# Attention's row maximum from the rounded parts of q and k, two heads at a time in row bands of the TensorE array

## The reference

```
qkv = h @ w_qkv + b_qkv                      # h: normalised and modulated x
q, k, v = rope(split(qkv)) per head          # (2, 16, 2048, 32) each
attn = softmax(q @ k^T / sqrt(32), axis=-1)  # 2048 x 2048 for each of 32 heads
out = attn @ v ;  x = x + out @ w_ao + b_ao
x = x + swiglu(norm2(x) @ w_fc + b_fc) @ w_fo + b_fo
```

## Time and profile before

| | |
|---|---|
| median of three runs | 3860.85 us |
| profiled execution, first to last instruction | 3862.3 us |
| granted TensorE clock, mean | 0.937 |
| up to the start of stage B | about 438 us |
| stage B ahead of its first product with v | 438 to 516 us |
| stage B, 32 units | 516 to 2535 us |
| stages C and D | 2535 to 3862 us |

### The profile page before, as it was taken

How to read it: one execution, slowest core, us unless ns; L and a number is a source line. 1 busy time by engine, 2 the same in 40 slices (tenths; PEclk the granted TensorE clock), 3 DMA queues, 4 the chain that set the end, 5 groups by cost and what they waited for, 6 DMA issues and landing times. The chain is left out here.

```text
span 3862.3 us, 54952 instructions
## 1 busy us (share of the span) xinstructions
PE 3485.2 (90%) x16467; PEld 2120.3 (55%) x16467; DVE 2194.5 (57%) x3311; ACT 1586.2 (41%) x2851; POOL 1691.7 (44%) x506
## 2 busy tenths in 40 slices
PE   6888699999999999999999999966399999799999
PEld 5666444444344443443443444445388888688887
DVE  2888577777677776777776767745422222221222
ACT  1433135555565555565655555523321111211111
POOL 0222247677777776777776767744200000100000
PEclk9999789999999999999999999987699999899999
DMA  4444421121210302112112031057531211322120
GB/s 172 139 140 145 127 65 26 45 52 32 65 32 24 73 26 58 39 27 70 29 29 68 25 71 28 25 175 245 174 117 49 82 43 55 98 98 76 47 83 22
DMA packets 154291, 289.31 MB, mean 75 GB/s; under 512 B 22410, under 2 KB 39930, under 8 KB 148606
## 3 DMA queue, kind: packets, MB, share of 16 engines
q1 hardware_dynamic: 139700, 250.89, 22.0%
q10 hardware_dynamic: 10512, 22.81, 1.8%
q0 software_dynamic: 3840, 12.59, 1.1%
HBM read 183.83 MB, written 102.27 MB: 74 GB/s over the span
## 5 line engine op out<-in xcount | busy, mean ns | idle before, releaser
L688 DVE TENSOR_REDUCE b_mpart<-b_m 128x1 f32<-128x512 f32 x2127 | 1334.5, 683 | 515.0 <-PE b_m L754 514.0
L675 POOL TENSOR_TENSOR b_acc<-b_acc,b_pt 128x2048 f32<-128x2048 f32 x288 | 1320.7, 4586 | 360.2 <-ACT b_pt L642 349.8
L642 ACT ACTIVATE b_pt<-b_s 128x512 f32<-128x512 f32 x2048 | 1118.6, 595 | 766.5 <-PE b_s L779 738.7
L779 PE MATMUL b_s<-b_qs,b_ks 98*128 98x512 f32 x2050 | 898.2, 438 | 89.8 <-ACT b_pt L642 75.1
L754 PE MATMUL b_m<-b_ks,b_qs 96*128 96x512 f32 x2127 | 828.0, 436 | 46.4 <-issue 20.5
L779 PEld LDWEIGHTS b_s<-b_qs,b_ks 98*128 98x128 f32 x2050 | 398.1, 194 | 691.6 <-ACT b_pt L642 605.8
L754 PEld LDWEIGHTS b_m<-b_ks,b_qs 96*128 96x128 f32 x2127 | 410.6, 201 | 307.1 <-DVE b_mpart L688 201.2
L844 PE MATMUL b_o<-b_pt,b_vg 128*32 128x512 f32 x4096 | 557.5, 617 | 0.0
L1184 DVE SCALAR_TENSOR_TENSOR d_uf<-d_a,keep_chan,d_sg 128x512 f32<-128x512 f32 x128 | 96.0, 750 | 578.4 <-PE d_a L1212 578.4
L1136 POOL DMA_DIRECT2D d_raw<-in_w_fc x32 | 24.0, 754 | 591.4 <-POOLq L1061 495.7
L1155 ACT ACTIVATE d_sg<-d_g,keep_chan 128x512 f32<-128x512 f32 x128 | 88.1, 688 | 419.3 <-PE d_g L1212 419.3
(11 more groups left out here) (130 smaller groups left out, 3781.6 us busy)
## 6 DMA issues: line engine op xcount, KB each, us to landing
b_ks<-scratch_qk_hi SPq DMA_DIRECT2D x18, 1024.0 KB, 14.1
b_qs<-scratch_qk_hi SPq DMA_DIRECT2D x68, 256.0 KB, 4.4
scratch_qk_hi<-a_q_hi SPq DMA_DIRECT2D x64, 256.0 KB, 2.5
scratch_qk_lo<-a_q_lo SPq DMA_DIRECT2D x64, 256.0 KB, 2.8
d_h_hi<-scratch_h_hi SPq DMA_DIRECT2D x16, 1024.0 KB, 7.4
d_h_lo<-scratch_h_lo SPq DMA_DIRECT2D x16, 1024.0 KB, 9.7
d_y<-scratch_y SPq DMA_DIRECT2D x16, 1024.0 KB, 8.4
b_ks<-scratch_qk_lo SPq DMA_DIRECT2D x9, 1024.0 KB, 13.1
```

Of the source, the lines that this page charges most:

```text
L642: act.activation(pt[:, kt % RING, h, :], ps_s[:, i % LEAD, :], ACT.Exp, scale=SCALE).then_inc(p_ready, 1)
L675: pool.tensor_tensor(sums[:], a, pt[:, kt % RING, :, :], ALU.add).then_inc(pool_added, 1)
L688: dve.tensor_reduce(mpart[slot][:, i // 4, i % 4:i % 4 + 1], ps_m[:, i % EARLY, :], AX.X, ALU.max).then_inc(max_done, 1)
L779: pe.matmul(ps_s[:, i % LEAD, :], ks[kslot][0:QR, h, kt * P:(kt + 1) * P], qs[qslot][0:QR, h, :], start=True, stop=True).then_inc(st_done, 1)
```

## The change

The maxima are computed from `qk_hi` alone: 32 rows of the array for a head and not 96. Since the four heads' rows of `qk_hi` lie side by side on 128 partitions, two heads' matmuls are issued one after the other in two bands of 32 rows. Both write a PSUM bank of their own, and one DVE instruction reduces both banks (128 x 2 x 512). What was 64 items a unit is now 32 (letter `M`).

- New tiles: `kn` (keys, rounded part, two slots) and `qn` (queries, rounded part, four slots), loaded by `load_group_hi` and `load_queries_hi`. The tile `qs` has two slots and not four.
- The four banks of the maxima are two pairs (`PAIRS = 2`).
- `ORDER` is new: nearly all steps are `sMsdMss`, `TURN` is 9 and not 12.
- POOL adds one key tile less, PE takes it: a `d` in seven steps of a unit and not in six (0, 2, 4, 7, 10, 12, 15 where it was 0, 2, 4, 7, 10, 13).
- On SP, `load_queries` goes to the end of a unit's body; the new loads stand at the start of it, ahead of the group's loads.

```diff
-BY_POOL = [0, 1, 2, 4, 5, 7, 8, 10, 11, 13, 14]
+BY_POOL = [0, 1, 2, 4, 5, 7, 8, 10, 12, 13]
...
-        FIVE, FOUR, TURN = "smsdmmmsms", "smsdmmsms", 12
-        ORDER = ([FOUR, FIVE] + [FOUR] * (TURN - 2)) + ["smsdmsmst"] + [FOUR] * (NK - 1 - TURN)
+        PLAIN, TURN = "sMsdMss", 9
+        ORDER = [PLAIN] * TURN + ["sMsdsst", "MsMsdMss"] + [PLAIN] * (NK - 2 - TURN)
...
+            def load_group_hi(G, i):
+                sp.dma_start(f32(kn[i][:]), scratch["qk_hi"][1, G]).then_inc(kn_in[i], 16)
+
+            def load_queries_hi(G, c, i):
+                sp.dma_start(f32(qn[i][:]), scratch["qk_hi"][0, G, :, c * TB:(c + 1) * TB]).then_inc(qn_in[i], 16)
...
             def body(u, pair, j):
-                sp.wait_ge(st_done, STEPS * (u + 1))
-                load_queries((2 * pair + (j + 2) // 4) % NG, (j + 2) % 4, (j + 2) % 4)
+                load_queries_hi((2 * pair + (j + 3) // 4) % NG, (j + 3) % 4, (j + 3) % 4)
                 if j % 4 == 0:
+                    load_group_hi((2 * pair + j // 4 + 1) % NG, (j // 4 + 1) % 2)
                     sp.wait_ge(pv_done, NK * u + RING)
                     load_group((2 * pair + j // 4 + 1) % NG, (j // 4 + 1) % 2)
...
+                sp.wait_ge(st_done, STEPS * (u + 2))
+                load_queries((2 * pair + (j + 2) // 4) % NG, (j + 2) % 4, j % 2)
...
             def maxima(n, slot, lo, hi):
+                parts = mpart[slot].rearrange("p (h s) k -> p h s k", h=GH)
                 for i in range(lo, hi):
+                    g, half = i // 2, i % 2
                     dve.wait_ge(max_ps, ITEMS * n + i + 1)
-                    dve.tensor_reduce(mpart[slot][:, i // 4, i % 4:i % 4 + 1], ps_m[:, i % EARLY, :], AX.X, ALU.max).then_inc(max_done, 1)
+                    dve.tensor_reduce(parts[:, 2 * half:2 * half + 2, g // 4, g % 4], ps_m[:, 2 * half:2 * half + 2, :],
+                                      AX.X, ALU.max).then_inc(max_done, 1)
...
-                    h, s, k = i // 16, i // 4 % 4, i % 4
-                    pe.wait_ge(max_done, ITEMS * (n + 1) + i + 1 - EARLY)
-                    if i == EARLY - 1:
+                    g, half = i // 2, i % 2
+                    s, k = g // 4, g % 4
+                    pe.wait_ge(max_done, ITEMS * (n + 1) + i + 1 - PAIRS)
+                    if i == 1:
                         pe.wait_ge(mlo_ready, n + 1)
-                    pe.matmul(ps_m[:, i % EARLY, :], qs[qslot][0:KR, h, s * P:(s + 1) * P],
-                              ks[kslot][0:KR, h, k * TB:(k + 1) * TB], start=True, stop=True).then_inc(max_ps, 1)
+                    for h in (2 * half, 2 * half + 1):
+                        last = pe.matmul(ps_m[:, h, :], qn[qslot][h * HD:(h + 1) * HD, s * P:(s + 1) * P],
+                                         kn[kslot][h * HD:(h + 1) * HD, k * TB:(k + 1) * TB], start=True, stop=True)
+                    last.then_inc(max_ps, 1)
```

More of the change, by code:

```diff
@@ L488, in stage_b @@
         ks = [m.sb(f"ks{i}", [QR, GH, T], F32R) for i in range(2)]
-        qs = [m.sb(f"qs{i}", [QR, GH, TB], F32R) for i in range(4)]
+        qs = [m.sb(f"qs{i}", [QR, GH, TB], F32R) for i in range(2)]
+        kn = [m.sb(f"kn{i}", [P, T], F32R) for i in range(2)]
+        qn = [m.sb(f"qn{i}", [P, TB], F32R) for i in range(4)]
         vg = [m.sb(f"vg{i}", [P, NK, P]) for i in range(2)]
@@ L509, in stage_b @@
          recip, on_ready, ohi_ready, olo_ready, o_stored, pool_added, ones_ready, m_out, d_out, dcol_in, r_out, r_in) = (m.sem(n) for n in names)
-        ITEMS = GH * SUB * 4
-        FIVE, FOUR, TURN = "smsdmmmsms", "smsdmmsms", 12
-        ORDER = ([FOUR, FIVE] + [FOUR] * (TURN - 2)) + ["smsdmsmst"] + [FOUR] * (NK - 1 - TURN)
-        PLAN = [o.count("m") for o in ORDER]
+        ITEMS = SUB * NJ * 2
+        PLAIN, TURN = "sMsdMss", 9
+        ORDER = [PLAIN] * TURN + ["sMsdsst", "MsMsdMss"] + [PLAIN] * (NK - 2 - TURN)
+        PLAN = [o.count("M") for o in ORDER]
         AHEAD = sum(PLAN[TURN:])
-        assert sum(PLAN) == ITEMS and PLAN[TURN] < EARLY
+        assert sum(PLAN) == ITEMS and PLAN[TURN] == 1
         D_PREV, D_ACC = 0, 2
@@ L577, in spread_denominators @@
                                  scratch["d"][1, h:h + 1].broadcast_to([HD, TB])).then_inc(r_in, 16)
+            load_queries_hi(0, 0, 0)
+            load_group_hi(0, 0)
+            for c in range(1, 3):
+                load_queries_hi(0, c, c)
             load_queries(0, 0, 0)
@@ L603, in _ @@
             for i in range(2):
-                sp.wait_ge(q_in[i], 48 * (UNITS // 4 + 1))
+                sp.wait_ge(q_in[i], 48 * (UNITS // 2 + 1))
+            for i in range(3):
+                sp.wait_ge(qn_in[i], 16 * (UNITS // 4 + 1))
             sp.wait_ge(k_in[0], 48 * (NG // 2 + 1))
+            sp.wait_ge(kn_in[0], 16 * (NG // 2 + 1))
             sp.wait_ge(v_in[0], 16 * (NG // 2 + 1))
@@ L766, in operands @@
             def operands(j, pair):
-                pe.wait_ge(q_in[j % 4], 48 * (2 * pair + j // 4 + 1))
-                pe.wait_ge(k_in[j // 4 % 2], 48 * (pair + j // 8 + 1))
+                pe.wait_ge(qn_in[j % 4], 16 * (2 * pair + j // 4 + 1))
+                pe.wait_ge(kn_in[j // 4 % 2], 16 * (pair + j // 8 + 1))
             def turn_max(n):
                 pe.wait_ge(mneg_ready, n + 1)
-                pe.transpose(ps_m[0:GH * SUB, EARLY - 1, 0:P], mneg[:], ident[:]).then_inc(mT_ps, 1)
+                pe.transpose(ps_m[0:GH * SUB, LAST, 0:P], mneg[:], ident[:]).then_inc(mT_ps, 1)
             def scores(n, kslot, qslot, i):
@@ L815, in body @@
                             if i == STEPS:
+                                pe.wait_ge(q_in[nq], 48 * (4 * pair + nj // 2 + 1))
+                                pe.wait_ge(k_in[nk], 48 * (pair + nj // 8 + 1))
                                 pe.wait_ge(m_in[nj % 2], 16 * (4 * pair + nj // 2 + 1))
@@ L821, in body @@
                             i += 1
-                        elif what == "m":
+                        elif what == "M":
                             if kt < TURN:
-                                maxima(u + 1, nk, nq, at, at + 1)
+                                maxima(u + 1, nk, nj % 4, at, at + 1)
                             else:
```

22 lines of the change are left out of this document (12 added, 10 removed).

## The result

The changed kernel takes 4736.94 us (median of four runs, 4713.32 to 4808.79), the kernel before 3861.01 us (3857.38 to 3866.62): 1.2246 times as long, 95% interval 1.221 to 1.2282. The direction was right, the size was not: 876 us where 146 were forecast, and the time lies far outside the range.

A forecast was written before the change was run, and what follows sets the result against it. PE's row of matmuls was taken to bound a unit. +4.5 us a unit over 32 units (+144), DMA +12 and -10 ahead of the units gave +146 us, so 4005 us; range 3745 to 4115.

The forecast's parts named there:

- The bound, the steps of 3.10 and 4.25 us, and the 6.4 us of stalls a unit: In the units: PE's matmuls set plain steps at 3.10 us, denominator steps at 4.25; stalls and slow clock add 6.4.
- A pair costs 0.63 us, since the shape change empties the array: Pairs on PE: 0.63 us each against 0.47 for two singles, +0.16; 32 pairs a unit, +5.1 us.
- Rival A: Pairs on PE: bands of rows cost no change of shape; -83 us, 3778 us in all; chance 0.28.
- B: Pairs on PE: shape change costs and the second band's load waits for the first; 4112 us; chance 0.11.
- the slow clock follows. I leave 3.5 of the 4.0 us: Behind the division, step 9: PE held over 2 us, then slow clock; 3.5 of 4.0 us stay, -0.5 a unit.
- The seventh `d`, +37 us: In the units: one more step with denominators on PE, +1.15 us a unit; nothing gained from POOL's relief.
- DVE 1.2 us a reduction and hidden: DVE in the units: a reduction of twice the length takes near 1.2 us, 38.4 a unit, hidden by PE.
- 10 us less ahead of the units: Ahead of the units: maxima start some 15 us sooner, DVE 2 us less, pairs due 7 more; -10 us.
- DMA, 12 us: Units that load a group: new loads queue ahead, delaying the denominators' reciprocal; 1.5 us each for eight units, +12 us.
- Rival C: PE saves and DVE's full banks vanish; the 4.0 us behind the division fall to 1; 3700 us; chance 0.06.

The follow-up runs named there:

- e12: Kernel before with the output's division and remainder both on POOL instead of DVE, SP sending the maxima ahead of the output; 3713.72 us, 0.9619 of before.
- e1: Changed kernel with each pair's matmuls on all 128 rows, queries padded with zeros for the other heads, so no shape change; 3983.45 us, 1.0316 of before.
- e7: Changed kernel with the two matmuls of every pair issued twice, in the same bands of 32 rows; 4994.33 us, 1.257 of before.
- e8: Changed kernel with bands of 64 rows for the pairs, queries padded with zeros for the neighbour head; 4307.12 us, 1.1015 of before.
- e4: Changed kernel with DVE's division in four pieces of 128 columns, one after each of steps 9 to 12; 4091.97 us, 1.0482 of before.
- e6: Kernel before with only POOL's list of key tiles changed: seven steps with denominators on PE instead of six; 3884.91 us, 1.0063 of before.
- e11: Changed kernel with the division on POOL instead of DVE, SP sending the maxima ahead of the output; 4047.44 us, 1.0334 of before.
- e3: Changed kernel with both pairs of a step side by side (sMMsdss for sMsdMss), half the excursions to bands; 4226.48 us, 1.0942 of before.
- e2: As e1, with a tiny 32-column matmul ahead of every pair, so two shape changes a pair on full rows; 4187.55 us, 1.0847 of before.
- e9: As e1, with the second pair of a step between the last two scores (sMsdsMs for sMsdMss); 3986.57 us, 1.0322 of before.

## Why the prediction was wrong

- *The bound, the steps of 3.10 and 4.25 us, and the 6.4 us of stalls a unit*: right; e12 removes 4.9 of the 6.4.
- *A pair costs 0.63 us, since the shape change empties the array*: right. Forecast 0.86 us from scores to scores, measured 0.85; 3.4 and 4.4 us a step, measured 3.47 and 4.37. Changing to bands of rows costs what changing to bands of columns does, where matmuls of full rows take 0.70 from scores to scores. The Trainium skill, "TensorEngine Tiling (Array Packing)", Tiling Modes, says that changing the tiling mode drains TensorE; the 0.85 us agree with it. Rival A and the gain are out. So is B: loads and matmuls of the two bands run side by side. (B's sum has a slip: 0.10 x 32 x 32 is 102 us, not 107.) The plain step's 0.07 us above the forecast lie at its last two scores, whose record is 0.83 us, not 0.73; a wait for an exponential fits, but is not shown.
- *"the slow clock follows. I leave 3.5 of the 4.0 us"*: this step failed. The stall was forecast at over 2 us and is 1.69. What failed is the term for the slow clock behind it: 3.5 us a unit rest on the silent assumption that the clock comes back as soon as in the kernel before. That was read from a trace in which nearly every matmul outside the column bands fills 96 or 98 rows, and the clock was down for 3 to 10 us at a time. With bands of 32 rows it was down for 360 us the first time and for 1992 us in all. The size: a unit came to 90.4 us where the forecast has 68.0 (67.6 and the DMA term), 22.4 x 32 = 717 us, nearly the whole miss. The clock alone accounts for about that much. A unit of nine plain steps and seven with denominators is 107.7 us at half clock and 61.8 at full, so 1992 us at half clock cost some 850, an estimate, and the forecast had 112 for it, the stall included. e1 shows that it is the bands that keep the clock down, e7 and e8 that the rows they fill have a part in it, e4 that a stall starts it. Why bands of few rows keep it down stays open.
- *The seventh `d`, +37 us*: 24 in e6.
- *DVE 1.2 us a reduction and hidden*: 1.224, hidden.
- *10 us less ahead of the units*: the first product with v starts at 505.8 for 516.3, 10.5 us less.
- *DMA, 12 us*: not told apart. In e4 the reciprocal of a unit that loads a group waited 8.0 to 8.4 us (786, 1329 and 1925 us) for 4.63 in the earlier trace rows, and PE 5.12 for 1.97 in the one compared. That is some 3 us more for such a unit instead of 1.5, about 25 us for eight of them, an estimate. With bands it is also the second place where the clock falls for long.
- *Rival C*, that the stall behind the division shrinks and the bands pay: e4 and e11 took the stall at step 9 away and came out 4.8 and 3.3% slower.
- The range was worked out from the cost of a shape change alone. Its upper end should have held the case that the clock does not recover: the rows at half clock would have priced it (at half clock a plain step came to 5.92 us, 1.7 times its 3.47), and the chance that the clock treats the new matmuls otherwise was not zero.

## What to carry to other kernels

Before matmuls are cut into bands of few rows, look at the granted clock and at every stall of a few us: this kernel recovered its clock within 3 to 10 us with full rows and took up to 360 with bands, and at half clock a step took 1.7 times as long. A pair in bands that stands alone between full-row work cost more than two matmuls of full rows (0.85 us from scores to scores for 0.70), since the array changes its shape on both sides; four in four bands cost less than four (0.86 for 1.17, e3). So band matmuls belong side by side, in as many bands as there are. And a DVE operation on two SBUF tensors beside long POOL operations was priced by POOL's instruction, not by its own size: cutting it into pieces multiplied the wait, and with both such operations on POOL (e12) it was gone.

## What the runs showed of the hardware

- The granted clock over the units was 0.95 or 0.96 with maxima of 96 to 128 rows, also with two shape changes a pair (before, e1, e2, e9); 0.80 with two bands of 64 rows; 0.82 with four bands of 32 at once; 0.65 to 0.67 with two of 32, streamed once or twice. The longest stretch at half clock was 10 us in the first group, 109, 48 and 256 to 362 in the others. Either level held for long with bands of 32 rows: from 516 us on e4 ran four units at 1.00 with the same matmuls on PE that the changed kernel ran at 0.50. Zeros in the stationary operand did not stand in the way: three quarters of e1's rows for the maxima are zeros.
- A change between full rows and bands of 32 rows costs as one to bands of columns (0.86 us worked out from those, 0.85 measured): scores, pair, scores take 0.85 us at full clock and 1.45 at half, where two full-row matmuls between the scores take 0.70. Four matmuls in four bands of 32 rows take 0.51 us together (e3).
- DVE's product of two SBUF tensors of 128 x 128 took 0.27 us alone and up to 4.60 beside POOL's additions; a subtraction of 128 x 512 took 0.69 and up to 4.17. On POOL both kinds take 1.28 us. DVE's reductions out of PSUM took 0.65 to 0.69 us in the kernel before, beside POOL's additions or not. The Trainium skill, "SBUF — State Buffer", Who interferes with whom, calls the port pair that VectorE and GpSimd share an exclusive lock; this case's runs agree, with the numbers above.
